# Graph network on one core: the last two edge passes also wait for a group gathered further on

## What is computed

```python
x = _layernorm(x + _L0_gnn_ref(x, edge_index, 12500, L0_gnn_W))            # softmax over edges, one head
x = _layernorm(x + _L1_gnn_ref(x, src, dst, L1_gnn_W_n, ...))               # softmax over edges, four heads, then an MLP
x = _layernorm(x + _L2_gnn_ref(x, edge_index, L2_gnn_W, L2_gnn_b))          # plain sum over edges
x = _layernorm(x + _L3_gnn_ref(x, edge_index, edge_weight, L3_gnn_We1, ...))
# the edge part of the last two:
out      = segment_sum(h[src] * norm[:, None], dst)                         # layer 3 of the four
messages = gelu(concat([hidden[src], hidden[dst], edge_weight]) @ We1 + be1) @ We2 + be2
agg      = segment_sum(messages, dst)                                       # layer 4 of the four
```

## Time and profile before

| | us |
|---|---|
| median of 3 runs | 8522.44 |
| lowest and highest run | 8519.18, 8523.58 |
| span of the profiled execution | 10211.6 |
| POOL busy in it | 6159.7 (60%) |
| DVE busy in it | 5157.6 (51%) |
| PE busy in it | 5172.9 (51%) |
| ACT busy in it | 2350.8 (23%) |

### The profile page before, as it was taken

The page is one execution under the profiler, slowest core; times in us unless marked ns, Lnnn a source line. Parts: engine busy times, 40 slices in busy tenths (PEclk is TensorE's granted clock), DMA queues, the critical chain, the costliest instruction groups (busy, mean ns, idle before and its releaser), DMA issues. The chain is left out here.

```text
span 10211.6 us, 117807 instructions
## 1 busy us (share of the span) xinstructions
PE 5172.9 (51%) x26943; PEld 4434.7 (43%) x27385; DVE 5157.6 (51%) x11737; ACT 2350.8 (23%) x7991; POOL 6159.7 (60%) x6684
## 2 busy tenths in 40 slices
PE   1544444447365666666673323333345565666655
PEld 1434433435254555555552222222244555555553
DVE  4644544546466666666652222222245555555556
ACT  1212211224244444444460000000021111111114
POOL 5666666662566555555516666666656666666664
PEclk9556556667677777777786656555576766666677
DMA  4222222222444444444421111111123333333331
GB/s 110 46 46 47 46 46 46 47 46 86 100 101 99 99 98 98 98 98 98 99 68 47 46 47 46 47 46 46 46 62 109 100 101 101 102 100 102 101 100 43
DMA packets 869663, 769.76 MB, mean 75 GB/s; under 512 B 385028, under 2 KB 727929, under 8 KB 868606
## 3 DMA queue, kind: packets, MB, share of 16 engines
q0 software_dynamic: 230416, 528.66, 20.4%
q1 hardware_dynamic: 626235, 228.48, 9.4%
q10 hardware_dynamic: 12344, 5.06, 0.2%
HBM read 707.24 MB, written 54.30 MB: 75 GB/s over the span
## 5 line engine op out<-in xcount | busy, mean ns | idle before, releaser
L1007 POOL DMA_INDIRECT rows_h<-t_d,idx x1563 | 1482.3, 948 | 1024.9 <-issue 396.3
L581 POOL DMA_INDIRECT rows_sum<-t_d,idx x1563 | 1474.7, 944 | 962.8 <-issue 453.5
L581 POOL DMA_INDIRECT rows_mlp<-t_d,idx x1548 | 1468.7, 949 | 834.1 <-remote 419.0
L1007 POOL DMA_INDIRECT rows<-t_d,idx x1477 | 1396.7, 946 | 812.6 <-issue 409.7
L1152 PEld LDWEIGHTS pn_h<-S_h,rows_h 128*128 128x128 f32 x6252 | 1098.1, 260 | 258.5 <-issue 223.2
L1152 PE MATMUL pn_h<-S_h,rows_h 128*128 128x128 f32 x6252 | 1141.6, 348 | 124.8 <-issue 110.3
L1047 ACT ACTIVATE rows_h<-rows_h,wc_h 128x64 f32<-128x64 f32 x4688 | 1135.9, 334 | 17.1 <-issue 7.0
L772 DVE TENSOR_TENSOR big<-big,pn_sum 128x512 f32 x391 | 269.2, 689 | 1687.0 <-remote 1535.6
L620 PE MATMUL pre_mlp<-dw_mlp,ST_mlp 128*128 128x128 f32 x3126 | 674.5, 379 | 475.8 <-DVE ST_mlp L59 185.3
L627 PE MATMUL pn_sum<-zb_sum 128*128 128x512 bf16 x325 | 175.4, 540 | 1294.4 <-DVE big L772 1089.9
L620 PEld LDWEIGHTS pre_mlp<-dw_mlp,ST_mlp 128*128 128x128 f32 x3126 | 591.2, 280 | 528.5 <-issue 513.8
(11 more groups left out here) (361 smaller groups left out, 8634.5 us busy)
## 6 DMA issues: line engine op xcount, KB each, us to landing
dw_mlp<-bd_d SPq DMA_DIRECT2D x1563, 64.0 KB
frow_mlp<-t_d ACTq DMA_DIRECT2D x1920, 0.5 KB
frow_h<-t_d SPq DMA_DIRECT2D x1792, 0.5 KB
lrb_h<-lrrow_d SPq DMA_DIRECT2D x196, 128.0 KB
lrb_mlp<-lrrow_d SPq DMA_DIRECT2D x98, 256.0 KB
rows_h<-t_d,idx POOLq DMA_INDIRECT x1563
dw_h<-xp_d SPq DMA_DIRECT2D x1563, 3.0 KB
rows_sum<-t_d,idx POOLq DMA_INDIRECT x1563
```

What stands on the lines that cost most here:

```text
L581: e.indirect_dma_start(rows[:, g % NR, j, :], None, table, bass.IndirectOffsetOnAxis(ap=idx[:, b, t:t + 1].bitcast(I32), axis=0)).then_inc ...
L1007: e.indirect_dma_start(rows[:, g % NR, j, :], None, table, bass.IndirectOffsetOnAxis(ap=idx[:, b16, t:t + 1].bitcast(I32), axis=0)).then_i ...
```

## The change

Each group's placing in the third pass, and each group's expansion and finishing in the fourth, gets one more wait: for the landing of the group that stands five (`sum`) or four (`mlp`) further on. For the last five or four groups of a pass there is no such group, and no wait. No instruction is moved and none but the waits is added.

```diff
+TRAIL = dict(sum=5, mlp=4)
...
+        def paced(e, g):
+
+            if g + TRAIL[mode] < GR:
+                sg, ng = gathered(g + TRAIL[mode])
+                e.wait_ge(sg, ng)
+
...
                 e.wait_ge(s_st, g + 1)
+                paced(e, g)
                 for j in range(SIZE[g]):
                     last = e.matmul(pre[g % 2][:, j, :], ST[:, g % 2, j, :], dw[:, g % ND, j, :], start=True, stop=True)
...
                 else:
                     sg, ng = gathered(g)
                     e.wait_ge(sg, ng)
+                    paced(e, g)
                 for j in range(SIZE[g]):
                     x = rows[:, g % NR, j, :]
...
                 sg, ng = gathered(g)
                 e.wait_ge(sg, ng)
+                paced(e, g)
                 b, q = divmod(g, NQ)
```

## The result

| | before, us | changed, us |
|---|---|---|
| median | 8523.01 (4 runs) | 8719.97 (4 runs) |
| lowest, highest | 8519.18, 8524.53 | 8714.46, 8725.28 |
| ratio | | 1.0233 [1.022, 1.0245] |
| span of the profiled execution | 10211.6, and 8535.0 when repeated | 8717.5 |

What follows compares the result with a forecast made beforehand. The prediction took POOL's back-to-back gathers to bound the kernel, steady state costing nothing; run-offs of 7.6 + 13.6 = 21 us added to 8522.4 gave 8543.6 us, own range 8536 to 8554, 8-in-10 range 8470 to 8580.

Steps and rivals of the forecast that it cites:

- Steady state, fourth pass: Fourth pass: place(g) follows the landing of g+5; after 4.0 us of expansion and placing, 7 us remain for the landing.
- Cost: nothing: Verdict on the fourth pass's steady state, as on the third's: the new waits add no time there.
- The third pass: Third pass: steady state costs nothing, 9 us being left for the landing; the run-off at its end costs 7.6 us.
- The run-off of the fourth: End of the fourth pass: groups still undone when the last group lands cost 13.6 us.
- The reading of the timed runs: Unprofiled, POOL never waits for the ring in the last two passes; other engines work directly behind the landing rows.
- the sum of 8696: Gathers back to back, 7689 us, plus 1007 us outside the four passes, without ring waits; set against the timed median 8522.
- The rule of the Trainium skill: DVE and GpSimd share a locked port pair, so moving DVE's work between gathers could gain; counted as worth nothing.
- Nothing to measure: Rival, 13%: engines are already five or more groups behind the gathers in timed runs, waits already fulfilled; 8522 (+-8) us.
- Faster: Rival, 25%: pacing ends the bursts and with them the late counts, removing ring waits; about 8450 us.
- The ring has no slack left: Rival, 12%: five of eight slots stay filled, so counts over 7 to 9 us late cost time; about 8600 us.

Runs made afterwards that it cites:

- mlp=3: The changed kernel with the fourth pass waiting three groups on, not four: 8550.6 us, 1.0037 against the kernel before; 1.0021 with late counts.
- nine slots: The changed kernel, five and four groups on, with nine slots in the ring of rows instead of eight: 8550.5 us, 1.0036 against the kernel before.
- the turned order: The changed kernel with all waits, PE's fourth-pass loop running place(i-1) ahead of expand(i+1): 8562.09 us, 1.0030 against the kernel before at 8536.70.
- the wait left out: The changed kernel without the new wait in expand, finish keeping its own: 8553.97 us, 1.0021 against the kernel before at 8536.70.
- mlp=5: The kernel before with waits in the fourth pass alone, five groups on, with late counts: 11894.94 us against 10104.89, 1.1774.
- mlp=4: The kernel before with waits in the fourth pass alone, four groups on: 8715.78 us, 1.0231; with late counts 1.0001.

## Why the prediction was wrong

**The step that failed** is "Steady state, fourth pass", where it says that PE runs expand(g+1) ahead of place(g), so that place(g) follows the landing of g+5. It follows that of g+6. The 11.3 us from the last gather to POOL's need are 6.3 us there, and by the prediction's own durations, 4.0 us for expansion and placing, 2.3 us are left for a landing that takes 2.6 to 3.3, and in one group of nine up to 4.7. "Cost: nothing" should have read "nothing at full clock, some 1 us a group at half clock". Measured were 175 us in 387 groups, 0.45 us each, and 173 / 186 = 0.9 us at each wait behind a placing at the lower clock. `mlp=3`, nine slots, the turned order and the wait left out each took it away, and `mlp=5` multiplied it. The order could be read in the loop's two lines.

**The third pass** was right: the steady state costs nothing (ring waits none, 1951.3 us against 1954.4 with gathers 3 ns longer and 1950.9 in the kernel that is paced in the fourth pass alone), and the run-off 7.4 us, predicted 7.6.

**The run-off of the fourth** was right: 14.4 us, predicted 13.6.

**The reading of the timed runs** was right in what the sum used, that they hold no ring wait; the repeated profile has none in the last two passes. Outside the four passes it has 823 us and not 1007, which is why the sum of 8696 stood above the median. That a profile as such looks otherwise was wrong: late counts are in timed runs too.

**The rule of the Trainium skill** was weighed wrongly. "By rule or by row the steady state is worth nothing" took a spacing of DVE's work to be neutral. In the paced fourth pass it moved one DVE instruction onto the starts of gathers: 10.6 us with `mlp=3`. In the changed kernel itself the gathers take 1471.3 us against 1466.5 to 1468.2, so it is 3 to 5 of the 175 us. The widest gather in the earlier trace rows, 1192 ns beside a median of 944, was the sign; the prediction took 1061, the widest of the third pass, for that of all.

**The rivals.** "Nothing to measure" fell: with prompt counts the engines are not five groups behind but directly behind the landing. "Faster" fell: with late counts, neither the change's parts nor its weaker forms are faster. Half of its mechanism was right, as the last section shows: pacing made the latest counts less late, and POOL waited as long as before. "The ring has no slack left" named the right resource and the wrong trigger. It wanted counts 7 to 9 us late and took its price from the third pass; no late count was needed, and only the fourth pass pays. By its own rate, the executions with late counts should have been the worst hit, and with `mlp=4` or less they lost at most 0.2%.

## What to carry to other kernels

Before a wait is tied to a landing, write down for each engine what the loop really issues between this wait and the release of the ring slot, with its lag, and take the durations at the lower clock. Here 6.25 us stood against 6.9. Take the landing at its longest too, not at its median. When a profile's span doesn't agree with the timed runs, get a second profile before arguing from its waits. A paced loop fixes the phase between engines, so a DVE instruction that disturbs a gather may do it every time.

## What was not expected of the hardware

**TensorE's counts can come late.** The same kernel takes 8519 to 8537 us on two chips and 10105 to 10228 us on three, timed and profiled alike. In the latter the increments of matmuls arrive up to 20 us after the last matmul, as in the earlier trace rows. What brings it about is open. Within a chip all executions were alike; whether the profile of 10211.6 us and the timed runs of 8522 beside it come from one chip is not on record. All four passes are longer with late counts.

**Pacing changes how late they are.** In the third pass an add, which waits for the count, starts at most 23.1 to 23.5 us behind the group's last matmul in the six profiles with late counts that leave this pass unpaced, and at most 10.2 to 10.6 us in the five that pace it. POOL's "remote" waits there stay the same, 281 to 296 us and 275 to 301. In the fourth pass of `mlp=5` 19 of 20 adds start within 0.4 us and there is no "remote" wait at all, with late counts in the third pass of the same execution. So the lateness hangs on how the engines are timed, and why is open.

**A gather's lengthening beside DVE.** A gather that starts while the ST write runs, and more than 0.13 us before its end, takes longer by the rest of that instruction less some 0.13 us (0.12 to 0.13 in 104 gathers with `mlp=3`); 28 that start less than 0.1 us after the write do not. In the changed kernel 172 gathers take over 960 ns, but only 28 of them start beside the write; 142 of the others have it start 0.3 to 0.5 us into them and are lengthened by some 0.035 us at the median. In the fourth pass with `mlp=3` the gathers take 10.6 us more than in the unpaced one.
